# Two-layer graph network kernel: the second layer's block 0 is summed beside the messages, and each projection step sums the next block

## The chip, the cores and the metric

One core of one Trainium2 chip runs the whole program. The time is the device time of one execution in microseconds. The kernel before takes 2986.62 us (median of three runs, 2985.55 to 2993.79).

## The reference, cut to what matters

The program takes 3125 nodes with 256 features and 100,000 edges sorted by destination, and runs two layers. The part that the change touches is in the second layer:

```python
# layer 1, graph part: messages from each edge's source, summed at its destination
h_src = h * norm_src[:, None]
msg = h_src[src]
agg = jax.ops.segment_sum(msg, dst, num_segments=n)
agg = agg * norm_dst[:, None]
out = jax.nn.elu(agg @ weight + bias)
# layer 1, mixer: q, k, v of every node, k-phi^T v summed over all nodes, then per node
q, k, v = x @ Wq + bq, x @ Wk + bk, x @ Wv + bv
kv = jnp.einsum('blhd,blhe->bhde', phi(k), v)
```

Then each node's row goes through the mixer's output projection, a norm, a feed-forward, a norm and the sum with the graph part, and at the end through two of eight experts.

## The kernel before, in words

The nodes are cut into NB = 25 blocks of B = 125, and five blocks (G = 5) make a step, so there are NS = 5 steps. The sum over edges is a dense product: for each destination block, layer 0 has left a table of edge counts between that block and all 25 source blocks (`counts`, 781 KB a block). A block's sum is 25 source blocks by 3 matmuls, since a message is held as three bf16 parts (`part0`, `part1`, `part2`) that add up to the f32 value. These 75 matmuls (`aggregate`, layer 1) accumulate in one PSUM bank, `ps_agg`. POOL loads the count tables into two buffers in turn (`adjacency_in`, `adj1`). After them comes the tail of the block, one round here: POOL's `gather` waits until the last block's tail was used (`tail_free`), loads one tile of edges, says `tail_known`, and fetches the source rows by an indirect load; DVE's `tails` makes a one-hot table from that tile's destinations (`tail_oh_full`); TensorE multiplies the two (`oh_tail`, `xg`), closes the bank (`agg_full`), and ACT's `keep_aggregate` copies the bank out, frees it (`agg_free`) and stores it.

Between the first layer's experts and the second layer's mixer stand two stages:

- **Messages.** ACT, DVE and POOL make the normalised rows and the messages, step by step. ACT says `msg_full` after each step, and POOL, which makes the second and third part of a message (`message_parts`), says `parts_made`. TensorE has no work there but the first transposes.
- **Projection loop.** TensorE's `project1(s)` transposes the five tiles of step s, makes q, k and v (20 matmuls of 512 columns and 20 of 256 in f32 passes), sums block s, and then adds this step's k-phi and v products to `ps_kv` (20 passes, called kv products below). DVE's `project1` adds the biases, and with ACT's Exp makes phi of k (`phi_full`), then the block's tail one-hot, then phi of q, which SP stores (`queries_out`, semaphore `q_free`). ACT's `project1` copies the transposed tiles out of PSUM and runs the Exp.

Each engine runs its instructions in the order in which they are written, so a wait holds back everything behind it. Blocks 0 to 4 are summed in the five projection steps and block 5 (NQ - 1) behind the loop. Then the mixer begins: its place "rows" sums the first half of block 6, and TensorE waits for DVE's `v_full`, which DVE gives after the step's rows and the seven bias rows are loaded (`l_bc`). SP issues these seven loads only once DVE has said `loop_done`, and DVE says that after `q_free` of step 4 and the closed `ps_kv`:

```python
            take(dve, k4_used)
            take(dve, q_free, 16)
            take(dve, sums_full)
            dve.sem_inc(loop_done, 1)
```

Of the kernel before, what the change touches and what calls it, by code (L numbers as in the profile page):

```python
# [27 lines left out]
N, E, D = 3125, 100000, 256  # L28
B = 125
NB = N // B  # L30
# [7 lines left out]
MAXT = NT  # L38
# [7 lines left out]
G = 5  # L46
NS = NB // G
# [17 lines left out]
NQ, NL = NS + 1, 3  # L65
# [3 lines left out]
def take(eng, sem, n=1):  # L69

    eng.wait_ge(sem, n)
    eng.sem_clear(sem)
# [19 lines left out]
def program(nc, a, out):  # L92
    ctx = ExitStack()
    with ctx:
# [10 lines left out]
        ps_agg, ps_kv = banks[0], banks[7]  # L105
# [10 lines left out]
        agg_rows1 = nc.dram_tensor("agg_rows1", (N, D + 1), F32).ap()  # L116
# [29 lines left out]
        tail_n = sb("tail_n", [1, NB], I32)  # L146
# [8 lines left out]
        xg = sb("xg", [B, NB + 1, D + 1])  # L155
        oh_tail, row_tail, col_tail = sb("oh_tail", [B, B]), sb("row_tail", [B, B]), sb("col_tail", [B, NB])
# [579 lines left out]
        def _(pe):  # L736
# [85 lines left out]
            def aggregate(b, par, layer, before, groups=ALL, first=False, last=False, nth=None):  # L822
# [26 lines left out]
                if groups[-1] == GR - 1:  # L849
# [10 lines left out]
                    zero(ps_agg, 260 + NB, False, True).then_inc(agg_full, 1)  # L860

            def turn_slots(groups):

# [177 lines left out]
            def project1(s):  # L1041
# [13 lines left out]
                if s == 0:  # L1055
                    pe.wait_ge(parts_made, NS)
                aggregate(s, s % 2, 1, total, nth=s // 2)
                take(pe, phi_full)
# [12 lines left out]
            pe.wait_ge(l_w1, 48)  # L1071
            total = pe.value_load(cum_tab[0:1, NB:NB + 1], min_val=NB, max_val=MAXT * NB)
            for s in range(NS):
                project1(s)
            zero(ps_kv, 258, False, True).then_inc(sums_full, 1)
            pe.wait_ge(l_c, 16 * 7)
            aggregate(NQ - 1, (NQ - 1) % 2, 1, total, nth=(NQ - 1) // 2)

# [71 lines left out]
        def _(act):  # L1150
# [225 lines left out]
            for s in range(NS):  # L1376
                messages(s)
            with act.Fori(0, NS) as s:
                project1(s)
                keep_aggregate(s, agg_rows1)  # L1380
            act.wait_ge(l_c, 16 * 7)
            act.wait_ge(l_l1, 16 * 4)
            keep_aggregate(NQ - 1, agg_rows1)

# [56 lines left out]
        def _(dve):  # L1441
# [534 lines left out]

            def project1(s):

# [20 lines left out]
                dve.sem_inc(phi_full, 1)  # L1999
                tails(s, 1)  # L2000
                take(dve, q_free, 16)
# [21 lines left out]
            dve.wait_ge(head_stored, 48)  # L2023
            with dve.Fori(0, NS - 1) as s:
                project1(s)
            dve.wait_ge(nodes_stored, 32)
            dve.sem_inc(rowb_used, 1)
            project1(NS - 1)
            take(dve, k4_used)
            take(dve, q_free, 16)  # L2030
# [10 lines left out]
            chain.restart()  # L2041
            tails(NQ - 1, 1)

# [153 lines left out]
```

## Time and profile before

| what | value |
|---|---|
| runs | 2986.62, 2993.79, 2985.55 us |
| the profiled execution's own time | 2994.02 us |
| its span in the trace | 2992.4 us |
| granted TensorE clock, mean over the span | 0.872 of full speed |
| DVE busy | 1159.4 us, 39% |
| ACT busy | 1103.8 us, 37% |
| POOL busy | 542.8 us, 18% |
| DMA | 202.07 MB, 68 GB/s over the span |

Times in the trace count from the span's start. A row of the timeline holds instructions that follow each other, with the time of the first, their busy time together and, in brackets, how long the engine was idle before and who released it. The messages stage runs from 1752 to 1824 us, the projection loop to 1972, and block 5 and the first half of block 6 follow until 1991.

### The profile page before, as it was taken

How to read it: one execution, taken by the hardware profiler on the slowest of the kernel's cores; microseconds unless marked ns; L12 is line 12 of the kernel's file. 1: busy time of each engine (PE TensorE's matmuls, PEld its weight loads, DVE VectorE, ACT ScalarE, POOL GpSimd, SP SyncE). 2: the span in 40 equal slices, each digit the busy share in tenths (PEclk: the TensorE clock that was granted, in tenths of full speed). 3: DMA queues.
4: the chain of work that ended last, by engine and by line, in shares of the span. 5: the costliest groups of instructions: out<-in, count | busy, mean ns of one | idle time of the engine just before them, and what ended most of it. 6: DMA issues, size and time to landing. Idle time of an engine off the chain costs nothing.

```text
span 2992.4 us, 40601 instructions
## 1 busy us (share of the span) xinstructions
PE 2385.0 (80%) x12530; PEld 1931.1 (65%) x12531; DVE 1159.4 (39%) x2546; ACT 1103.8 (37%) x2058; POOL 542.8 (18%) x470
## 2 busy tenths in 40 slices
PE   0777699989889889896679936888788887846887
PEld 0444588877777768775568834666666666635776
DVE  4444577754554544542100034332423334231111
ACT  3122477756555645561223333212222121112232
POOL 1520011100010100102122223010202021113454
PEclk9878799999888898997689977998798897867999
DMA  3321111110110110203332234331222223423443
GB/s 122 95 84 51 30 39 40 44 60 25 34 59 31 53 39 16 75 15 103 101 97 66 64 99 133 95 105 44 75 64 53 71 48 88 122 62 70 82 85 64
DMA packets 163999, 202.07 MB, mean 68 GB/s; under 512 B 55840, under 2 KB 134159, under 8 KB 163860
## 3 DMA queue, kind: packets, MB, share of 16 engines
q0 software_dynamic: 69408, 81.85, 11.8%
q1 hardware_dynamic: 82874, 107.64, 10.9%
q10 hardware_dynamic: 11578, 10.82, 1.1%
q8 instruction: 74, 1.21, 0.2%
q14 instruction: 65, 0.53, 0.1%
HBM read 108.51 MB, written 93.74 MB: 68 GB/s over the span
## 4 chain that ended last, share of the span: by engine, by line
PE 46%; DMA 35%; another core or an unknown queue 7%; ACT 3%; DVE 3%; issue 2%; SPq 2%; POOL 1%; ACTq 0%; DVEq 0%; POOLq 0%
PE bank L738 43%; DMA agg_rows<-agg_t 32%; PE bank L744 3%; POOL w_adj L583 1%; DMA arena<-agg_rows 1%; SPq L411 1%; DMA arena<-in_x 1%; ACT w_qc L1200 0%; DMA xg<-expert_rows 0%; ACT count_a L1200 0%; DMA feat<-row_hot 0%; ACT agg_t L1217 0%; DVE arena L1922 0%; ACT w_adj L1199 0%
## 5 line engine op out<-in xcount | busy, mean ns | idle before, releaser
L738 PE MATMUL bank<-xg,w_adj 125*125 125x256 f32 (+1 forms) x2500 | 583.8, 345 | 1.1 <-DMA w_adj<-counts 1.1
L738 PEld LDWEIGHTS bank<-arena,row_hot 128*125 128x125 f32 x3200 | 428.2, 200 | 87.9 <-issue 67.5
L738 PE MATMUL bank<-arena,row_hot 128*125 128x100 f32 x3200 | 435.6, 283 | 46.9 <-remote 19.6
L738 PEld LDWEIGHTS bank<-xg,w_adj 125*125 125x125 f32 (+1 forms) x2500 | 376.2, 169 | 24.7 <-DMA w_adj<-counts 1.3
L744 PE MATMUL bank<-ident,arena 125*128 125x125 f32 (+1 forms) x650 | 148.3, 355 | 304.2 <-remote 126.3
L738 PE MATMUL bank<-t,w_h 128*128 128x250 f32 (+1 forms) x1184 | 332.5, 435 | 24.4 <-remote 20.3
L744 PEld LDWEIGHTS bank<-ident,arena 125*128 125x128 f32 (+1 forms) x650 | 89.0, 175 | 358.0 <-issue 352.8
L1199 ACT ACTIVATE w_adj<-bank 125x200 f32<-125x200 f32 x400 | 217.3, 543 | 274.6 <-PE bank L738 266.2
L1603 DVE TENSOR_TENSOR row_hot<-iota_all,arena 128x2000 f32<-128x2000 f32 x100 | 223.8, 2238 | 233.7 <-PE bank L738 230.8
L738 PEld LDWEIGHTS bank<-t,w_h 128*128 128x128 f32 x1184 | 234.2, 203 | 120.0 <-issue 68.4
L738 PE MATMUL bank<-w_adj,arena 128*125 128x256 f32 x1024 | 239.9, 392 | 0.0
L1200 ACT ACTIVATE count_a<-bank 125x200 bf16<-125x200 f32 x208 | 227.6, 1094 | 4.0 <-issue 4.0
L738 PEld LDWEIGHTS bank<-w_adj,arena 128*125 128x125 f32 x1024 | 196.7, 196 | 29.7
L1200 ACT ACTIVATE w_qc<-bank 125x200 bf16<-125x200 f32 x192 | 210.1, 1094 | 0.0
L630 POOL DMA_DIRECT2D edge_tail<-in_edges x50 | 27.8, 555 | 823.4 <-PE bank L738 773.1
L738 PE MATMUL bank<-w_adj 125*125 125x256 bf16 x625 | 175.7, 281 | 0.0
L1157 ACT ACTIVATE t<-bank 128x250 f32<-128x250 f32 (+1 forms) x225 | 90.8, 403 | 185.7 <-PE bank L744 183.3
L664 POOL DMA_INDIRECT out_rows<-arena,ids_cur x60 | 119.8, 1997 | 154.4 <-DVEq L1889 119.4
L685 POOL DMA_INDIRECT sorted_in<-arena,pos_cur x75 | 94.4, 1259 | 242.4 <-DVEq L1845 221.4
L1180 ACT ACTIVATE arena<-bank,b_col 128x375 f32<-128x375 f32 (+1 forms) x160 | 83.0, 521 | 118.5 <-PE bank L738 118.4
L633 POOL DMA_INDIRECT xg<-feat,edge_tail x50 | 76.8, 1536 | 263.7 <-DMA edge_tail<-in_edges 156.3
L1263 ACT ACTIVATE arena<-bank,b_col 128x250 f32<-128x250 f32 x136 | 63.5, 469 | 157.3 <-PE bank L738 157.2
(330 smaller groups left out, 3021.2 us busy)
## 6 DMA issues: line engine op xcount, KB each, us to landing
w_adj<-counts POOLq DMA_DIRECT2D x25, 781.2 KB, 8.8
arena<-sorted_in SPq DMA_DIRECT2D x49, 251.0 KB
counts<-count_a SPq DMA_DIRECT2D x13, 781.2 KB
counts<-w_qc SPq DMA_DIRECT2D x12, 781.2 KB
arena<-rows_b SPq DMA_DIRECT2D x5, 1875.0 KB
w_adj<-in_L_ffn_Wd POOLq DMA_DIRECT2D x8, 1024.0 KB, 6.4
w_adj<-in_L_ffn_W POOLq DMA_DIRECT2D x16, 512.0 KB, 5.7
sorted_in<-pad_rows POOLq DMA_DIRECT2D x8, 878.4 KB, 16.8
```

The costliest lines, as they stand in the source:

```text
L411: sp.dma_start(x_big[:, 5 * i:5 * i + 5, :], xv[:, 5 * i:5 * i + 5, :]).then_inc(step_got[i], 16)
L633: pool.indirect_dma_start(xg[:, NB, 0:D], None, feat, bass.IndirectOffsetOnAxis(ap=idx_tail[:, 0:1], axis=0)).then_inc(tail_full, 16)
L664: pool.indirect_dma_start(out, rows_of, y_out[:, i, :], None, bounds_check=N - 1, oob_is_err=False, compute_op=ALU.add).then_inc(y_landed[ ...
L685: pool.indirect_dma_start(sorted_in, bass.IndirectOffsetOnAxis(ap=pos_cur[:, k, i:i + 1], axis=0), src[:, i, :], None).then_inc(scattered, 16)
L738: return pe.matmul(o, w, r, start=first, stop=last, skip_group_check=not check)
L744: return pe.transpose(ps[:, at:at + n], src, ident[0:n, 0:n])
L1157: chain(act.activation(t4[:, k:k + n, B * i:B * i + B], ps_t[i % 2][:, 0:n * B].rearrange("p (k n) -> p k n", k=n), ACT.Copy))
L1180: last = act.activation(ht[:, slot + j, lo:hi], ps_h[half][:, 0:hi - lo], func, bias=b(j))
L1199: act.activation(wide(adj[par], g), ps[:, :, 0, :, :], ACT.Copy)
L1200: last = act.activation(wide(count_cur[par], g), ps[:, :, 1, :, :], ACT.Copy)
L1263: act.activation(ht[:, j, 0:PT], ps_u[j % 4][:, 0:PT], ACT.Gelu, bias=b(e, j)).then_inc(unit_done[j % 4], 1)
L1603: tt(row_hot[:, k % 2, :, :], iota_all[:, :].unsqueeze(1).to_broadcast([128, GJ, B]), src[1].to_broadcast([128, GJ, B]), ALU.is_equal)
```

## The change

`first_sums` opens the sums' bank right behind the experts and sums block 0 source step by source step: it waits for `parts_made` of each of the five steps and issues the 15 matmuls of that step's five source blocks. `project1(0)` then begins. Behind its projections stands `first_tail`, which adds block 0's tail and closes the bank; then `project1(0)` sums block 1, and each further step s sums block s + 1. The block behind the loop is gone. ACT keeps two sums in step 0 and one in each later step, and DVE makes two tail one-hots in step 0. POOL and SP are unchanged.

```diff
+            def first_sums():
+                open_sums()
+                pe.wait_ge(adj_in[0], 16)
+                for s in range(NS):
+                    pe.wait_ge(parts_made, s + 1)
+                    for c in range(G * s, G * s + G):
+                        mm(ps_agg[0:B, 0:D + 1], adj1[0][:, c, 0:B], part0[:, c, :], False, False, False)
+                        mm(ps_agg[0:B, 0:D], adj1[0][:, c, 0:B], part1[:, c, :], False, False, False)
+                        mm(ps_agg[0:B, 0:D], adj1[0][:, c, 0:B], part2[:, c, :], False, False, False)
+                zero(ps_agg, 16, False, False).then_inc(adj_used[0], 1)
+
+            def first_tail(before):
+                n = pe.value_load(tail_n[0:1, 0:1], min_val=1, max_val=MAXT)
+                with pe.Fori(0, n) as c:
+                    take(pe, tail_oh_full)
+                    pe.wait_ge(tail_full, pe.snap((before + c + 1) * 16))
+                    mm(ps_agg[0:B, 0:D + 1], oh_tail[:, :], xg[:, NB, 0:D + 1], False, False, False).then_inc(tail_free, 1)
+                zero(ps_agg, 260 + NB, False, True).then_inc(agg_full, 1)
...
                 if s == 0:
-                    pe.wait_ge(parts_made, NS)
-                aggregate(s, s % 2, 1, total, nth=s // 2)
+                    first_tail(total)
+                aggregate(s + 1, (s + 1) % 2, 1, total, nth=(s + 1) // 2)
                 take(pe, phi_full)
...
+            first_sums()
             for s in range(NS):
                 project1(s)
             zero(ps_kv, 258, False, True).then_inc(sums_full, 1)
             pe.wait_ge(l_c, 16 * 7)
-            aggregate(NQ - 1, (NQ - 1) % 2, 1, total, nth=(NQ - 1) // 2)
...
-            with act.Fori(0, NS) as s:
+            project1(0)
+            for b in range(2):
+                keep_aggregate(b, agg_rows1)
+            with act.Fori(1, NS) as s:
                 project1(s)
-                keep_aggregate(s, agg_rows1)
+                keep_aggregate(s + 1, agg_rows1)
...
-            keep_aggregate(NQ - 1, agg_rows1)
...
-            with dve.Fori(0, NS - 1) as s:
-                project1(s)
+            project1(0)
+            tails(1, 1)
+            with dve.Fori(1, NS - 1) as s:
+                project1(s + 1)
             dve.wait_ge(nodes_stored, 32)
             dve.sem_inc(rowb_used, 1)
-            project1(NS - 1)
+            project1(NS)
...
-            tails(NQ - 1, 1)
```

How the instructions stand on TensorE is printed below; L72 is the line of a wait, and the semaphores that a row waits for are in brackets. The first place is the beginning of the stage, right behind the last expert. Before:

```order
1505 L738 MATMUL bank<-zero_r,zero_w 128x258
1506 L1072 TENSOR_LOAD cum_tab [waits w_qkv1_loaded]
1507 L1072 ISA x2
1508 L72 ISA [waits turned_ps_free0,messages1_full]
1509 L744 MATMUL bank<-ident,arena 128x125 x2
1510 L72 ISA [waits turned_ps_free1]
1511 L744 MATMUL bank<-ident,arena 128x125 x2
```

And with the change, where the last of the five groups of 15 (its first matmul waits for the parts) ends and the first transpose follows:

```order
1508 L72 ISA [waits agg_ps_free]
1509 L738 MATMUL bank<-zero_r,zero_w 128x285
1510 L738 MATMUL bank<-xg,w_adj 125x257 [waits message_parts_made,adjacency_in0]
...
1570 L738 MATMUL bank<-xg,w_adj 125x257 [waits message_parts_made]
...
1585 L738 MATMUL bank<-zero_r,zero_w 128x16
1586 L72 ISA [waits turned_ps_free0,messages1_full]
1587 L744 MATMUL bank<-ident,arena 128x125 x2
1588 L72 ISA [waits turned_ps_free1]
1589 L744 MATMUL bank<-ident,arena 128x125 x2
```

The transposes and projections of step 0 now stand behind all 75 matmuls of block 0, the last 15 of which wait for the last message parts.

The second place is the end of step 0's projections on TensorE, with the change. Before, the last projection (`w_qc,t`) was followed by the 75 matmuls of block 0, and its tail came behind them:

```order
1616 L738 MATMUL bank<-w_qc,t 125x256 x2
1617 L876 TENSOR_LOAD tail_n
1618 L876 ISA x2
1619 L877 UNCONDITIONAL_BRANCH
1620 L72 ISA [waits tail_onehot_full]
1621 L879 ISA
1622 L738 MATMUL bank<-xg,oh_tail 125x257 [waits tail_rows_full]
1623 L877 REGISTER_ALU
1624 L877 COMPARE_AND_BRANCH
1625 L738 MATMUL bank<-zero_r,zero_w 128x285
1626 L72 ISA [waits agg_ps_free]
1627 L738 MATMUL bank<-zero_r,zero_w 128x285
```

Two waits now stand between the projections and the next 75 matmuls: that for the tail's one-hot and that for the bank.

The third place is the end of the loop on TensorE, behind the last kv products. Before, block 5 stood between them and the mixer (its 75 matmuls follow the last row here):

```order
2117 L738 MATMUL bank<-arena 128x129 x10
2118 L738 MATMUL bank<-zero_r,zero_w 128x258
2119 L72 ISA [waits agg_ps_free,w_c_loaded]
2120 L738 MATMUL bank<-zero_r,zero_w 128x285
```

With the change the mixer's loop begins there, and its first work is the first half of block 6:

```order
2204 L738 MATMUL bank<-arena 128x129 x10
2205 L738 MATMUL bank<-zero_r,zero_w 128x258
2206 L1162 UNCONDITIONAL_BRANCH [waits w_c_loaded]
2207 L72 ISA [waits agg_ps_free]
2208 L738 MATMUL bank<-zero_r,zero_w 128x285
2209 L830 ISA
...
2243 L72 ISA [waits vector_stage_full]
2244 L72 ISA [waits turned_ps_free0]
2245 L744 MATMUL bank<-ident,arena 128x125 x2
```

## Rows read from the trace of the kernel before

**Rows 1.** Page, part 1: busy time, share of the span, instructions.

```profile
PE 2385.0 (80%) x12530; PEld 1931.1 (65%) x12531; DVE 1159.4 (39%) x2546; ACT 1103.8 (37%) x2058; POOL 542.8 (18%) x470
```

**Rows 2.** Timeline of PE, steps 0 and 1: start us, us, instructions [idle <-releaser].

```profile
1776.97 1.09 PE L744 MATMUL bank<-ident,arena 125*128 125x125 f32 x4 [29.51 <-ACTq L1356]
1819.94 2.05 PE L744 MATMUL bank<-ident,arena 125*128 125x125 f32 x6 [41.88 <-ACTq L1159]
1821.78 15.05 PE L738 MATMUL bank<-w_qc,t 128*125 128x512 f32 x40
...
1845.49 0.70 PE L738 MATMUL bank<-xg,oh_tail 125*125 125x257 f32 x2
...
1846.34 2.50 PE L738 MATMUL bank<-arena 125*128 125x129 f32 x20
1848.67 0.59 PE L744 MATMUL bank<-ident,arena 125*128 125x125 f32 x4
...
1852.58 14.83 PE L738 MATMUL bank<-w_qc,t 128*125 128x512 f32 x40
```

**Rows 3.** Timeline of POOL, the last of the five message parts.

```profile
1821.80 2.52 POOL L616 TENSOR_TENSOR w_adj<-row_hot,xg 125x1280 bf16<-125x1280 f32 x1
```

**Rows 4.** Timeline of DVE in step 0, the tail's one-hot.

```profile
1843.55 0.29 DVE L1652 TENSOR_SCALAR oh_tail<-iota_all,dst_tail 125x125 f32<-125x125 f32 x1
```

**Rows 5.** Three stretches: length, busy by engine (instructions), PEclk, DMA share, GB/s.

```profile
1777.00:1819.00 42.00, 1.07 (x4) 0.68 (x4) 27.91 (x53) 25.88 (x49) 26.72 (x17) 0.50 0.34 120
...
1822.00:1827.00 5.00, 5.00 (x10) 2.45 (x10) 1.04 (x2) 0.38 (x1) 2.32 (x1) 0.62 0.35 124
...
1985.20:1990.70 5.50, 5.45 (x33) 5.21 (x33) 0.00 (x0) 0.00 (x0) 1.16 (x1) 0.69 0.34 118
```

**Rows 6.** Timeline of PE, step 4, block 5 and the mixer's beginning.

```profile
1945.51 14.63 PE L738 MATMUL bank<-w_qc,t 128*125 128x512 f32 x40
...
1969.64 2.50 PE L738 MATMUL bank<-arena 125*128 125x129 f32 x20
...
1982.02 0.69 PE L738 MATMUL bank<-xg,oh_tail 125*125 125x257 f32 x2 [1.05 <-DVE oh_tail L1652]
...
1983.80 0.29 PE L738 MATMUL bank<-zero_r,zero_w 1*128 1x285 bf16 x1 [0.87 <-ACTq L1218]
...
1993.71 1.09 PE L744 MATMUL bank<-ident,arena 125*128 125x125 f32 x4 [3.05 <-remote]
```

**Rows 7.** Timeline of POOL, gather for block 1, and landing of the indirect loads.

```profile
1846.96 0.58 POOL L630 DMA_DIRECT2D edge_tail<-in_edges  x1 [7.25 <-PE bank L738]
1852.33 1.24 POOL L633 DMA_INDIRECT xg<-feat,edge_tail  x1 [4.78 <-remote]
...
DMA to landing us min/median/max: 4.2/5.3/8.7
```

**Rows 8.** Timelines of DVE and SP between step 4 and the mixer.

```profile
1967.49 1.49 DVE L2003 SCALAR_TENSOR_TENSOR count_a<-arena 125x1280 f32<-125x1280 f32 x1 [0.19 <-remote]
...
1993.52 1.49 DVE L2060 TENSOR_TENSOR arena<-arena,bias 125x1280 f32<-125x1280 f32 x1 [11.77 <-DMA arena<-rows_b]
...
1969.12 0.27 SPq L506 DMA_DIRECT2D rows_b<-count_a  x1
1978.13 0.28 SPq L519 DMA_DIRECT2D bias<-in_L_gnn_bias  x1
...
1982.62 2.63 SPq L519 DMA_DIRECT2D bias<-in_L_mix_ln_b  x1
```

**Rows 9.** Timelines of PE and DVE, step 2 and the beginning of step 3.

```profile
1879.25 0.59 PE L744 MATMUL bank<-ident,arena 125*128 125x125 f32 x4
...
1891.27 8.00 PE L738 MATMUL bank<-w_qc,t 128*125 128x512 f32 x24 [1.01 <-DVE arena L1984]
...
1911.11 0.59 PE L744 MATMUL bank<-ident,arena 125*128 125x125 f32 x4
...
1888.01 1.49 DVE L2003 SCALAR_TENSOR_TENSOR count_a<-arena 125x1280 f32<-125x1280 f32 x1 [13.65 <-remote]
```

More of the change, by code:

```diff
@@ L1975, in nodes1, with project1 @@
                 chain.restart()
-            def project1(s):
+            def project1(b):
                 take(dve, k4_used)
@@ L1999, in project1 @@
                 dve.sem_inc(phi_full, 1)
-                tails(s, 1)
+                tails(b, 1)
                 take(dve, q_free, 16)
```

## The prediction

> **What bounds the kernel now.** I read the busy times first: TensorE is busy 80% of the span, the next engine 39% [rows 1]. So TensorE is the first suspect, but a share is a mean over stages, and the change moves work between two of them. The timeline of TensorE around them tells more. In the messages stage it stands still: two tiles are transposed at 1776.97, and the third waits 41.88 us, until 1819.94 [rows 2]. The projections of step 0 then run from 1821.78 to 1836.83, block 0's 75 matmuls fill the time to its tail at 1845.49, the kv products follow at 1846.34, and step 1 begins at 1848.67 [rows 2]. Inside the loop TensorE is the bound. A block costs 1845.49 - 1836.83 = 8.7 us with its opening, 0.115 us a matmul.
>
> At the loop's end I looked at who releases TensorE, since removing work there pays only if TensorE is late. Its projections of step 4 end at 1945.51 + 14.63 = 1960.14, the kv products at 1972.1, block 5 runs to its tail at 1982.02, half of block 6 from 1983.80, and then it is idle for 3.05 us, until the mixer's first transpose at 1993.71 [rows 6]. The rows of DVE and SP name the real chain: DVE ends phi of q at 1968.98, SP stores it at 1969.12, the store has landed by 1978.1, when SP issues the first of seven bias loads; the last is issued from 1982.62 to 1985.25, and DVE starts the mixer at 1993.52, 0.19 us before TensorE [rows 8]. DVE's row names an old load of rows as releaser, which was issued long before; the bias loads are what can have come last. So from the end of step 4's projections to the mixer there are 1993.71 - 1960.14 = 33.6 us whatever TensorE does, and block 5 lies in their shadow.
>
> **The change, part by part.** I follow TensorE from the last message parts to the end of step 0. Before, that end was 1848.67.
>
> 1. *Block 0 beside the messages.* The first 60 matmuls fall in the 41.88 us of idleness and cost nothing; if that cover were gone they would cost 60 x 0.115 = 6.9 us. The last 15 wait for POOL's last part, ready at 1824.32 [rows 3]. They take 15 x 0.115 = 1.7 us at full clock, 3.5 us at the half clock (1.2 GHz) that TensorE was granted through this stage, 0.50 [rows 5]. I take the level that the row shows, 3.5: 1827.8.
> 2. *Transposes.* They now stand behind this. In step 1 it took 1852.58 - 1848.67 = 3.9 us from the first transpose to the first projection, because ACT loads its Copy table only once a tile is there [rows 2]. In step 0 that was hidden, now it is not. With transposes at half clock (1.09 us for four against 0.59) I take 4.2: 1832.0.
> 3. *Projections.* 15.0 us, as in both steps [rows 2]: 1847.0 instead of 1836.83.
> 4. *The tail's one-hot.* DVE made it at 1843.84, 7.0 us after the last projection, since phi of k and two Exp stand before it [rows 2, 4]. Before, the 75 matmuls covered this. Now nothing does, for the tail comes first: 1854.0. The order of work can't shorten this wait, since DVE's own order is unchanged up to there.
> 5. *Tail, closing, and the bank.* Block 1 needs the same bank, and ACT must copy it out first. From tail to reopening it took 1983.80 - 1982.02 = 1.8 us [rows 6]: 1855.8. ACT is free by then; its Exp is what the one-hot waited for.
> 6. *Block 1.* 8.7 us at full clock. After the pause in point 4 I expect part of it at half clock: after the pause before block 6, 33 matmuls took 5.5 us at a mean clock of 0.69 [rows 5], where 33 x 0.115 = 3.8 would do. So +1.7: 1866.2.
> 7. *Block 1's tail rows.* POOL may fetch them only after block 0's tail is used, at 1854.7. From there the row shows 0.8 us to the edge load, 5.4 to the indirect load, and 5.3 (median, 4.2 to 8.7) to its landing [rows 7]: 11.4 us, so 1866.1, level with point 6. Between no wait and 3.4 us I take 0.5, near the median: 1866.7. Before, a whole step lay between two tails.
> 8. *Tail and kv products*, 1848.67 - 1845.49 = 3.2 us [rows 2]: step 0 ends at 1869.9, which is **21.2 us later**.
> 9. *Steps 1 to 4.* The same instructions in the same order, with the next block's count table and tail. Count tables are issued at the same distance, a step ahead. One stall goes: before, DVE waited 13.65 us for an old store, until 1888.01, and TensorE 1.01 us for DVE, so that the step from 1879.25 took 31.9 us where the loop's first full step took 30.6 [rows 2, 9]. That store waited behind SP's weight loads, which do not move, and DVE now reaches it some 20 us later. I take the whole difference, **-1.3 us**.
> 10. *Behind the loop.* Block 5's 75 matmuls, tail and reopening go, from 1972.1 to 1983.80, 11.7 us of TensorE. The chain of store, `loop_done` and bias loads is unchanged, so TensorE does half of block 6 and idles until 33.6 us after its projections: **0**. What may go is contention: block 7's table came in beside the last bias loads and will come earlier now. At most 2 us of the 8.3 us from the last bias issue to DVE's start [rows 8]; I count none and keep 2 for the range. Below zero it can hardly cost anything.
> 11. *ACT's and DVE's second pieces in step 0* (one more copy, one more one-hot) run while TensorE is in block 1, and POOL and SP issue what they did. The mixer's passes behind are the same work; nothing there waits for an absolute time. 0.
>
> Sum: 21.2 - 1.3 + 0 = **+19.9 us**. The profiled execution would take 2994.0 + 19.9 = 3013.9 us. It was 7.4 us above the median of the runs, so against the median the forecast is 2986.6 + 19.9 = **3006.5 us**, 0.7% slower. A difference under 0.3%, 9 us, can't be told from none here.
>
> The Trainium skill, DMA: Bandwidth & Descriptors, "Latency and other measured facts", gives some 2 us as a DMA's fixed cost. By that estimate block 1's rows would be there about 6 us after the first tail, and the sum would be 0.5 us smaller; the 5.4 and 5.3 us of the rows speak against it, and they hold.
>
> The Trainium skill, TensorE: Matmul & The Clock Gate, "Why this matters for your kernels", advises against gaps between bursts of matmuls, for the clock falls in them. That speaks against this change, which opens such a gap in point 4. The 1.7 us of point 6 come from the row of block 6, and the trace agrees with the rule there; without it the sum would be 1.7 us smaller.
>
> Bounds. Below: full clock in points 1, 2 and 6 makes 1.8 + 0.3 + 1.7 = 3.8 us less, of which the tail rows (11.4 us after the first tail) give back about 1.5, and 2 us of point 10: +15. Above: the lower clock through all projections of step 0. In 1822 to 1827, mostly at half clock, 10 matmul rows ran in 5 us [rows 5], against 40 in 15; that would be at most 10 us more, and tail rows 3.4 us late: +33.
>
> **The rivals.**
> - *Block 5 was on the path after all (slower by less than can be told).* If the mixer's first transpose waited for TensorE itself, the 11.7 us of point 10 would come back: 19.9 - 11.7 = +8.2, 2994.8 us, and with the lower bounds less. It decides if the chain from step 4's projections to DVE's start is shorter than 33.6 - 11.7 = 21.9 us. For it: TensorE was idle only 3.05 us there. Against it: DVE's and SP's rows add up without TensorE. Chance 0.09.
> - *Slower still, by clock and late rows.* Point 1's bursts keep the clock down through step 0's projections and block 1, and the indirect load lands late: +28, 3015 us. For it: half clock for 42 us. Against it: step 0's projections began at the lower level before, too, and still took 15.05 us [rows 2, 5]. Chance 0.12.
> - *The stages interleave as meant.* If DVE's one-hot and block 1's rows did not hold up TensorE, only the late start of the projections would be paid, 1832.0 - 1821.78 = 10.2 us, and with block 5's 11.7 and the 1.3 back it would be -2.8: 2983.8 us, no change. The Trainium skill, Perfetto Trace Analysis, "Optimization Strategy", says that interleaving stages with different limits may help; the time for it is this rival's. Against it stands the order of DVE: the one-hot comes after phi of k. Chance 0.03.
>
> **How the numbers follow.** The forecast itself, with bounds of +15 to +25, has 0.74, and 0.02 is left for a gain that no row shows. The range goes from 2997 to 3017: it leaves out the third rival, most of the first and the far end of the second, and takes in the run-to-run spread of some 4 us. Slower by over 0.3% is the forecast, the second rival and a part of the first: 0.88. Within 0.3%: 0.10. Faster: 0.02.
>
> **What would show it.** In the profile after: 15 matmuls on `xg,w_adj` after each message part; the first projection of step 0 near 1832 and its last near 1847; a pause of some 7 us on TensorE released by DVE's `oh_tail`, one of 0.9 us released by ACT, perhaps one by the tail rows; step 1 beginning near 1870; steps of 30.4 to 30.6 us; and after the loop a pause of 15 to 17 us before the mixer's first transpose (3.05 + 11.7, and what block 6 lost to its pause and the lower clock), still 33.6 us after step 4's projections. I am wrong if that last distance shrinks by over 3 us, or if step 0 ends before 1862.

## The result and the profile after

| | before | after |
|---|---|---|
| runs, median (lowest to highest) | 2988.51 us (2979.30 to 3001.97), 20 runs | 3001.89 us (2984.74 to 3011.39), 20 runs |
| ratio after to before, on record | | 1.0030 (95%: 1.0018 to 1.0043) |
| span of the profiled execution | 2992.4 us | 2999.6 us |
| granted clock, mean | 0.872 | 0.874 |

The changed kernel is slower, as forecast, but not by 19.9 us. The recorded ratio makes it 9.0 us (5.4 to 12.8). It isn't the quotient of the two medians, which lie 13.4 us apart, just beyond that interval; so read the size as some 9 to 13 us. The direction was right; half to two thirds of the amount came.

The spans can't be subtracted. In the changed kernel's execution the experts ended 10.8 us earlier than in that of before, at 1736.4 against 1747.2 us, though nothing there was changed. So I count from the end of POOL's last message part, 1824.32 before [rows 3] and 1810.81 + 2.51 = 1813.32 after, and cut at TensorE's first transposes:

| stretch | before | after | difference | forecast |
|---|---|---|---|---|
| last message part to step 1 | 24.35 | 47.01 | +22.66 | +21.2 |
| steps 1 to 3 | 92.80 | 82.82 | -9.98 | -1.3 |
| step 4 and loop's end, to the mixer | 52.24 | 49.29 | -2.95 | 0 |
| first two passes of the mixer | 29.91 | 33.76 | +3.85 | 0 |
| sum | 199.30 | 212.88 | +13.58 | +19.9 |

The first row is where the forecast looked, and it holds. The second and third are where it failed: each of steps 1 to 4 is some 3 us shorter (2.75 to 4.25), and the forecast had only 1.3 us for all of them, from one stall.

Timeline of TensorE after, from the last of the five groups of block 0 into step 1 (start, us, instructions, [idle <-releaser]); it answers to [rows 2]:

```profile
1813.42 0.69 PE L738 MATMUL bank<-xg,w_adj 125*125 125x257 bf16 x2 [7.13 <-POOLq L617]
...
1816.95 1.09 PE L744 MATMUL bank<-ident,arena 125*128 125x125 f32 x4
...
1820.16 13.90 PE L738 MATMUL bank<-w_qc,t 128*125 128x512 f32 x40
1842.40 1.21 PE L738 MATMUL bank<-xg,oh_tail 125*125 125x257 f32 x2 [8.34 <-DVE oh_tail L1675]
...
1844.75 0.41 PE L738 MATMUL bank<-zero_r,zero_w 1*128 1x285 bf16 x1 [0.79 <-ACTq L1239]
...
1857.14 0.70 PE L738 MATMUL bank<-xg,oh_tail 125*125 125x257 f32 x2 [1.53 <-DMA xg<-feat,edge_tail]
...
1860.33 0.59 PE L744 MATMUL bank<-ident,arena 125*128 125x125 f32 x4
1861.40 0.43 PE L744 MATMUL bank<-ident,arena 125*128 125x125 f32 x2 [0.49 <-ACTq L1180]
...
1862.96 13.14 PE L738 MATMUL bank<-w_qc,t 128*125 128x512 f32 x40
```

All three waits that the prediction named are there, in their order: the one-hot 8.34 us, the bank 0.79, the tail rows 1.53. But look at the last two rows. In step 1, TensorE pauses 0.49 us between its first transposes and the next, and the projections take 13.14 us; before, they took 14.83 [rows 2], behind a pause of 1.76:

```profile
1851.03 0.43 PE L744 MATMUL bank<-ident,arena 125*128 125x125 f32 x2 [1.76 <-ACTq L1159]
```

ACT's timeline says what the pause was. Before, in step 1:

```profile
1849.16 1.28 ACT L1157 ACT_TABLE_LOAD   x1 [2.16 <-PE bank L744]
1850.45 0.38 ACT L1157 ACTIVATE t<-bank 128x250 f32<-128x250 f32 x1
```

After, in steps 0 and 1:

```profile
1835.91 1.28 ACT L1385 ACT_TABLE_LOAD   x1 [15.04 <-DVEq L2018]
1837.20 2.43 ACT L1385 ACTIVATE arena<-arena 125x1280 f32<-125x1280 f32 x2
1844.16 0.39 ACT L1238 ACTIVATE agg_t<-bank 125x257 f32<-125x257 f32 x1 [4.53 <-DMA agg_rows<-agg_t]
...
1860.83 0.38 ACT L1178 ACTIVATE t<-bank 128x250 f32<-128x250 f32 x1 [2.17 <-PE bank L744]
```

Before, every step began with a load of ACT's table; after, there is one load in front of step 0's Exp, and none in steps 1 to 4. The listing of ACT's instructions shows the same thing. Before, the loop's body begins with the load (`1282 L1157 ACT_TABLE_LOAD`, the first row behind the loop's branch and its wait). With the change the row `1292 L1385 ACT_TABLE_LOAD` stands in step 0's peeled copy, and the loop behind `1304 L1402 UNCONDITIONAL_BRANCH` holds none. The page agrees, with four instructions fewer on ACT than in [rows 1] (2054 for 2058):

```profile
PE 2377.7 (79%) x12530; PEld 1926.4 (64%) x12531; DVE 1160.3 (39%) x2546; ACT 1100.6 (37%) x2054; POOL 544.4 (18%) x470
```

The pause fell by 1.27 us, about the load's length. The other 1.7 us lie in the projections, and the three stretches of step 1 before show why (length, busy by engine, PEclk, DMA share, GB/s):

```profile
1850.70:1852.50 1.80, 1.04 (x6) 0.59 (x6) 0.00 (x0) 1.01 (x4) 0.17 (x1) 1.00 0.34 119
1852.50:1857.00 4.50, 4.50 (x11) 2.42 (x11) 0.69 (x1) 0.64 (x2) 1.64 (x2) 0.62 0.70 201
1857.00:1867.00 10.00, 10.00 (x32) 5.74 (x31) 4.08 (x8) 0.00 (x0) 0.00 (x0) 1.00 0.42 126
```

Right behind the pause the granted clock fell to a mean of 0.62, so that most of 4.5 us ran at 1.2 GHz. After the change the clock stays at 1.00 there:

```profile
1862.00:1874.00 12.00, 11.73 (x38) 6.90 (x39) 4.39 (x8) 1.15 (x3) 1.82 (x2) 1.00 0.86 211
```

The Trainium skill, ScalarE: Activation LUTs, "What ACT_TABLE_LOAD costs", gives 1283 ns for the load and some 1380 ns for a drain, 2.66 us a switch. The trace agrees with the first, 1.28 us. It doesn't show the second: ACT had been idle before the load, and its next instruction begins 0.01 us behind it.

At the loop's end it went as forecast. TensorE, SP and DVE after:

```profile
1992.44 1.09 PE L744 MATMUL bank<-ident,arena 125*128 125x125 f32 x4 [17.41 <-remote]
...
1967.48 0.27 SPq L506 DMA_DIRECT2D rows_b<-count_a  x1
1976.81 0.28 SPq L519 DMA_DIRECT2D bias<-in_L_gnn_bias  x1
...
1982.57 2.82 SPq L519 DMA_DIRECT2D bias<-in_L_mix_ln_b  x1
...
1992.25 1.49 DVE L2084 TENSOR_TENSOR arena<-arena,bias 125x1280 f32<-125x1280 f32 x1 [13.73 <-DMA arena<-rows_b]
```

Step 4's projections end at 1958.91, and the mixer's first transpose follows 33.53 us later, against 33.6 before [rows 6, 8]. TensorE now idles 17.41 us where it idled 3.05. Block 5 was taken out of a shadow. Which transfer DVE waits for in the end isn't shown: its row names the load of the nodes' rows (`rows_b`), the prediction the bias rows.

### The profile page after: what moved, and what is told of

Its sections match the earlier page's. It is cut to its first block, busy times and chain, and to the rows that moved or that the text cites. A ratio compares the mean times of both kernels' runs of the same rounds, so it can differ in the third digit from the quotient of the medians.

```text
span 2999.6 us, 40584 instructions
## 1 busy us (share of the span) xinstructions
PE 2377.7 (79%) x12530; PEld 1926.4 (64%) x12531; DVE 1160.3 (39%) x2546; ACT 1100.6 (37%) x2054; POOL 544.4 (18%) x470
## 4 chain that ended last, share of the span: by engine, by line
PE 43%; DMA 36%; another core or an unknown queue 7%; ACT 5%; DVE 3%; issue 2%; SPq 2%; POOL 1%; ACTq 0%; DVEq 0%; POOLq 0%
PE bank L738 40%; DMA agg_rows<-agg_t 33%; PE bank L744 3%; SPq L411 1%; POOL w_adj L583 1%; DMA arena<-agg_rows 1%; ACT arena L1299 1%; ACT count_a L1221 0%; DMA xg<-expert_rows 0%; ACT w_qc L1221 0%; DMA feat<-row_hot 0%; ACT agg_t L1238 0%; ACT w_adj L1220 0%; DVE arena L1945 0%
## 5 line engine op out<-in xcount | busy, mean ns | idle before, releaser
L738 PE MATMUL bank<-xg,w_adj 125*125 125x256 f32 (+1 forms) x2500 | 590.7, 348 | 62.8 <-POOLq L617 62.8
L1284 ACT ACTIVATE arena<-bank,b_col 128x250 f32<-128x250 f32 x136 | 63.7, 471 | 156.6 <-PE bank L738 156.5
```

What stands on the lines that cost most here:

```text
L738: return pe.matmul(o, w, r, start=first, stop=last, skip_group_check=not check)
L1284: act.activation(ht[:, j, 0:PT], ps_u[j % 4][:, 0:PT], ACT.Gelu, bias=b(e, j)).then_inc(unit_done[j % 4], 1)
```

## The experiments

Each kernel was timed beside the kernel before on the same chip, in 6 to 12 executions; where one execution is said, there is no ratio. The medians of before were 2990.41, 2987.32 and 2986.64 us in the three series. "Step 0" stands for the stretch from the last message part to step 1's first transpose.

**Peeling ACT's loop alone, on the kernel before.** TensorE's order stays that of before.

```diff
-            with act.Fori(0, NS) as s:
+            project1(0)
+            keep_aggregate(0, agg_rows1)
+            with act.Fori(1, NS) as s:
                 project1(s)
                 keep_aggregate(s, agg_rows1)
```

> The kernel before, with nothing changed but ACT's projection loop: step 0 is written out ahead of the loop, which runs over steps 1 to 4. Theory: the loop then begins with the Exp table in place and ACT loads no table in steps 1 to 4, so the first transpose of a step is followed by its first projection after 2.6 us instead of 3.9, TensorE's pause falls from 1.76 to 0.5 us, its clock does not fall, the projections take 13.1 instead of 14.8 us, and a step takes 27.6 instead of 30.6 us: 12 us less in four steps, some 1 us in step 0, about 2975 us against 2988. Rival (the shorter steps of the change come from TensorE's order or from the tail one step ahead): steps stay at 30.6 us and the time at 2988.

Measured: 2986.04 us, ratio 0.9995 (0.9975 to 1.0015), no gain that can be told, where some 2975 was expected. The table loads of steps 1 to 4 are gone and steps 1 and 3 take 27.61 us, as with the change. But step 2 takes 40.21 us, which eats the gain. TensorE and DVE there, and SP's queue up to it:

```profile
1880.75 10.07 PE L738 MATMUL bank<-w_qc,t 128*125 128x512 f32 x24 [10.27 <-DVE arena L1986]
...
1877.48 1.49 DVE L2005 SCALAR_TENSOR_TENSOR count_a<-arena 125x1280 f32<-125x1280 f32 x1 [19.93 <-remote]
...
1822.91 31.87 SPq L497 DMA_DIRECT2D wn<-in_L_gnn_weight  x1
...
1865.24 14.32 SPq L506 DMA_DIRECT2D rows_b<-count_a  x2
```

DVE may write step 1's queries only once step 0's have been stored. SP issues that store behind seven weight loads, the first of which kept its queue 31.87 us. Counted from the last message part (1811.88 here), DVE went on after 65.6 us, and before, from 1888.01 [rows 9], after 63.7: an almost fixed time. Before, TensorE came late enough to lose only 1.01 us to it [rows 9]; here it begins step 2 4.4 us earlier and is 3 us faster inside it, and the stall ends 2 us later, so it loses 10.27. So the peeling is the cause of the shorter steps, and it doesn't pay by itself in this kernel; the change, which starts its steps some 20 us later, passes under the stall.

**The loads put back into the changed kernel.** One dummy operation leaves ACT with the Sqrt table before the loop, as the messages did.

```diff
                 keep_aggregate(b, agg_rows1)
+            table(ACT.Sqrt)
             with act.Fori(1, NS) as s:
```

> The changed kernel with ACT's Sqrt table loaded between step 0 and the loop, so that the loop is again entered with another table than it leaves. Theory: the load at the first copy of steps 1 to 4 is back, the steps take 30.6 us again, and the kernel is 12 us slower than the changed one: ratio to before 1.007, near the 19.9 us that were forecast. Rival (the load is not what made the steps shorter): steps stay at 27.6 us, ratio 1.003.

Measured: 3010.77 us, ratio 1.0062 (1.0040 to 1.0083), 18.5 us slower than before. The load is back in each step, the steps take 30.30, 30.45 and 30.56 us, and step 1's projections, behind a pause of 1.87 us, are slow again:

```profile
1874.00 1.28 ACT L1178 ACT_TABLE_LOAD   x1 [0.30 <-PE bank L744]
...
1877.63 14.24 PE L738 MATMUL bank<-w_qc,t 128*125 128x512 f32 x40
```

This is the kernel that the prediction had costed, and the 19.9 us of its sum lie inside the interval of what it measured (12 to 25 us). By stages it agrees too: from the last message part to the mixer's first transpose it took 187.9 us, 18.5 more than before. That a loop which is entered with one table and left with another needs a load in every pass is my reading of the two listings and of this pair of kernels; no row says it.

**Block 5's 75 matmuls left out of the kernel before.** Its sums are not computed.

```diff
-                        for c in range(NB * max(g - 1, 0) // 15, NB * g // 15):
+                        for c in range(0 if empty else NB * max(g - 1, 0) // 15, 0 if empty else NB * g // 15):
...
-            aggregate(NQ - 1, (NQ - 1) % 2, 1, total, nth=(NQ - 1) // 2)
+            aggregate(NQ - 1, (NQ - 1) % 2, 1, total, nth=(NQ - 1) // 2, empty=True)
```

> The kernel before without the 75 matmuls of block 5 behind the loop (its tail and its store stay, so the sums of block 5 are left out). Theory: the mixer's first transpose waits for the chain store, loop_done, bias loads, and stays 33.6 us behind the last projection of step 4, with TensorE idle some 8 us longer: same time as before. Rival (block 5 was on the path): 8.7 us less and the distance falls to 25 us.

Measured: 2990.02 us, ratio 1.0001 (0.9986 to 1.0017). Taking away 8.7 us of TensorE's work gains nothing; the wait for the tail's one-hot takes its place, and the mixer begins 35.3 us behind step 4's projections, not sooner than the 33.6 of before:

```profile
1969.35 1.22 PE L738 MATMUL bank<-xg,oh_tail 125*125 125x257 f32 x2 [9.41 <-DVE oh_tail L1652]
...
1982.92 0.64 PE L744 MATMUL bank<-ident,arena 125*128 125x125 f32 x4 [3.33 <-remote]
```

By itself this leaves the tail of block 5 in TensorE's way, and TensorE idle for 3.33 us only, as before. Together with the changed kernel, in which nothing of block 5 is left there and the distance is still 33.53 us, it refutes the rival with block 5 on the path.

**The changed kernel without block 0's tail product and one-hot.** The tail of block 0 is not added.

```diff
                 with pe.Fori(0, n) as c:
-                    take(pe, tail_oh_full)
                     pe.wait_ge(tail_full, pe.snap((before + c + 1) * 16))
-                    mm(ps_agg[0:B, 0:D + 1], oh_tail[:, :], xg[:, NB, 0:D + 1], False, False, False).then_inc(tail_free, 1)
+                    pe.sem_inc(tail_free, 1)
...
-                tails(b, 1)
+                if not isinstance(b, int) or b > 0:
+                    tails(b, 1)
...
             dve.wait_ge(head_stored, 48)
+            take(dve, tail_known)
             project1(0)
```

> The changed kernel with block 0's tail product and its one-hot left out (the tail rows are fetched and awaited as before). Theory: the pause of 8.3 us between step 0's projections and block 1 goes, and with it the lower clock in block 1 (2 us): step 0 ends 9 to 11 us sooner, the whole kernel is about as fast as before. Rival (the pause only hides another wait, for block 0's tail rows or block 1's): a wait of 5 us or more appears in its place and 3 us at most are gained.

Measured: 2991.29 us, ratio 1.0008 (0.9991 to 1.0025). Step 0 takes 42.38 us, 4.6 less than with the change. The 8.34 us of the one-hot gave way to another wait, for ACT's copy of the bank:

```profile
1838.50 0.29 PE L738 MATMUL bank<-zero_r,zero_w 1*128 1x285 bf16 x1
1844.60 0.41 PE L738 MATMUL bank<-zero_r,zero_w 1*128 1x285 bf16 x1 [5.81 <-ACTq L1238]
```

ACT's copy stands behind its table load and both Exp. The one-hot is only the last of two waits that end close together, and behind it 5.81 of its 8.34 us remain.

The last line of the edit costs time of its own. The word `tail_known`, which the one-hot no longer takes, is now taken ahead of all of DVE's work in step 0, so DVE stands still until the edge load of block 0 has landed. The projections wait 1.60 us for it and take 15.80 us where they took 13.90:

```profile
1829.52 0.07 DVE L2003 MEMSET arena<- 125x10 f32 x1 [28.10 <-remote]
```

So the 4.6 us are a lower bound for what this wait was worth; with the projections at 13.90 it would be 6.5, an estimate.

**The same, with ACT's copy of block 0's sums ahead of the two Exp.**

```diff
                 copy_turned(2)
+                if isinstance(s, int):
+                    keep_aggregate(0, agg_rows1)
                 for n in (1, 0):
...
-            for b in range(2):
-                keep_aggregate(b, agg_rows1)
+            keep_aggregate(1, agg_rows1)
```

> As e4 (block 0's tail product and one-hot left out), and ACT copies block 0's sum out before its two Exp of step 0 instead of behind them. In e4 TensorE waited 5.8 us for that copy. Theory: the pause between the projections of step 0 and block 1 falls to about 1 us, the clock stays up, and step 0 ends some 8 us sooner than in e4, 12 us sooner than in the changed kernel: some 3 us faster than before. Rival (block 1's tail rows, which come 11 us after the last use, bind next): 2 to 3 us of that are given back.

Measured: 2983.30 us, ratio 0.9990 (0.9964 to 1.0015). Step 0 takes 37.71 us, 9.3 less than with the change. The projections wait 2.71 us for DVE, again through the line with `tail_known`, part of them runs slower (17.80 us in all, for 13.90), and 0.78 us remain at the bank:

```profile
1834.44 9.70 PE L738 MATMUL bank<-w_qc,t 128*125 128x512 f32 x24 [2.71 <-DVE arena L2007]
...
1845.14 0.29 PE L738 MATMUL bank<-zero_r,zero_w 1*128 1x285 bf16 x1 [0.78 <-ACTq L1238]
```

With both waits away, the way from the last message part to the mixer's third transposition is 199.0 us, that of before 199.3. Step 0 is still 13.4 us longer than before (some 9.5 by estimate, with the projections at 13.90), since transposes and projections now stand behind the messages, and the shorter steps give back 12.9. So of the 22.7 us by which step 0 had grown, taking both waits away gave back 9.3 (13 by that estimate), and what is left and the shorter steps cancel. In time the kernel can't be told from before.

**Peeling with `loop_done` said earlier, on the kernel before.** DVE gives it right behind the last phi of q, ahead of its waits for the store and for `ps_kv`.

```diff
+            dve.sem_inc(loop_done, 1)
             take(dve, k4_used)
             take(dve, q_free, 16)
             take(dve, sums_full)
-            dve.sem_inc(loop_done, 1)
```

> The kernel before with ACT's loop peeled (as e1) and DVE's loop_done given before the three waits behind the loop, right after phi of q of step 4. Theory: SP issues the bias loads 9 us earlier, the chain that starts the mixer ends before block 5 and half of block 6 do, and the mixer's first transpose follows TensorE's own work, 30 us behind step 4's projections instead of 33.6 (e1: 34.4 with the last step): 3 to 4 us less than e1. Rival (the mixer waits for an old load of rows, as its row says, not for the biases): no change against e1.

Measured: 2978.67 us, ratio 0.9979 (0.9955 to 1.0003). From step 4's first transpose to the mixer's it took 51.13 us, no less than the 50.17 of the peeling alone: the stretch I had expected to shrink did not, since block 5's tail rows now came late. What did shrink is the mixer's first pass, 14.15 us for 17.72, and TensorE no longer idles before it; that the one comes of the other is my reading:

```profile
1968.36 1.22 PE L738 MATMUL bank<-xg,oh_tail 125*125 125x257 f32 x2 [5.32 <-DMA xg<-feat,edge_tail]
...
1977.57 0.59 PE L744 MATMUL bank<-ident,arena 125*128 125x125 f32 x4
```

**The same, with step 0's query store ahead of SP's weight loads.** This tests the account of the 10.27 us stall.

```diff
+            take(sp, q_full)
+            sp.dma_start(rows(rows_b[:, 2 * D:3 * D], 0), q1).then_inc(q_free, 16)
             sp.dma_start(wn[:, :, :], wview(a["L1_gnn_weight"])).then_inc(l_c, 16)
...
-            with sp.Fori(0, NS - 1) as s:
+            with sp.Fori(1, NS - 1) as s:
                 queries_out(s)
```

> As e5, and SP stores step 0's queries ahead of the seven weight loads instead of behind them. Theory: in e1 the table load was taken out of four steps, 12 us, but DVE's wait for that store grew and stopped TensorE for 10.3 us in step 2; with the store ahead, step 2 takes 27.6 us like the others instead of 40.2, and the kernel is some 12 us faster than e5 and 15 us faster than before, ratio 0.995. Rival (the store itself is slow, or the weight loads then hold back step 1's store by as much): a stall of 10 us moves to step 3.

Measured: 2961.81 us, ratio 0.9922 (0.9892 to 0.9951), some 23 us faster than before, and the fastest of all. Steps 1 to 3 take 27.61, 27.60 and 27.61 us: the stall in step 2 is gone. Step 2's projections on TensorE, and the store on SP:

```profile
1866.72 13.14 PE L740 MATMUL bank<-w_qc,t 128*125 128x512 f32 x40
...
1833.87 22.50 SPq L498 DMA_DIRECT2D rows_b<-count_a  x1
```

Even in front, the store keeps SP's queue 22.50 us, but now nobody waits for it, and the weight load behind it keeps the queue only 5.37 us: the long hold goes with the place in the queue, not with the weight load. Of the 23 us, the stretches of the table give 13.8 in the profiled execution (185.5 against 199.3 us). The rest lies outside them, where executions of one kernel differ by as much (below), and I can't assign it.

**A pause without a table.** The peeled kernel before, with a Copy of 1.25 us on an unused tile ahead of the first copy of each of steps 1 to 4 (one execution).

```diff
                     take(act, t_act[i % 2])
+                    if pause and i == 0:
+                        idle = cut(17800, 1250)
+                        chain(act.activation(idle, idle, ACT.Copy))
...
-                copy_turned(2)
+                copy_turned(2, pause=not isinstance(s, int))
```

> As e1 (no table load in steps 1 to 4), with one ACT copy of 125x1250 elements, some 1.2 us, put where the table load was: after the wait for the first transposed tile. Theory: the pause of TensorE alone costs the clock; the projections take 14.8 us again instead of 13.1 and steps 1, 3 and 4 take some 30.4 us, of which 1.3 are the pause and 1.7 the clock. Rival (the table load itself slows something else): steps take 27.6 + 1.2 = 28.8 us.

Measured: 2991.36 us. The pause on TensorE is 1.76 us again, in all four steps. Steps 1 and 3 take 28.88 and 28.89 us, 1.3 more than with no pause, and their projections run at full clock; in steps 2 and 4 the clock fell. TensorE in steps 1, 3 and 4, then, in a fence of their own, two stretches of step 1:

```profile
1846.97 0.43 PE L744 MATMUL bank<-ident,arena 125*128 125x125 f32 x2 [1.76 <-ACTq L1162]
...
1916.67 13.14 PE L738 MATMUL bank<-w_qc,t 128*125 128x512 f32 x40
...
1945.56 14.61 PE L738 MATMUL bank<-w_qc,t 128*125 128x512 f32 x39
```

```profile
1844.60:1848.40 3.80, 1.60 (x11) 0.92 (x10) 0.07 (x1) 2.46 (x5) 0.24 (x1) 1.00 0.34 120
1848.40:1852.40 4.00, 4.00 (x13) 2.23 (x13) 1.12 (x2) 0.69 (x2) 1.58 (x2) 1.00 0.64 184
```

So 1.3 us of the 3.0 are the pause, whether the clock falls or not. The other 1.7 are the clock's, and a pause of this length may cost them or not: it fell in every step of the kernels that had the loads, in two of four here, and in none whose pause was 0.49 us.

**Both kernels a second time** (one execution each, nothing edited), to see what repeats.

> The kernel before, unchanged, for a second trace. What the readings by stage rest on should repeat to some 1 to 2 us: 24.4 us from the last message part to step 1, 30.6 us a step with the table load, 52 us from step 4 to the mixer's first transpose; the rest of the spread between executions should lie ahead of the messages and behind the mixer's first pass.

> The changed kernel, unchanged, for a second trace: 47.0 us from the last message part to step 1, 27.6 us a step, 49.3 us from step 4 to the mixer's first transpose. If these repeat, the difference between the two kernels from the last message part to the mixer is 9.7 us, whatever the whole times of the two executions are.

Measured: 2966.54 and 2999.46 us. Step 0 took 24.33 and 45.81 us, the steps 30.58, 31.07, 30.58 and three times 27.6, the way from step 4 to the mixer 52.39 and 48.57. The mixer's first two passes took 29.93 and 32.67 us. Every stretch of the table repeats to 1.2 us, and this pair's sum is +11.0 us where the first pair's was +13.6. Outside the table nothing repeats so well. The same kernel before reached its last message part at 1824.3 us in one execution and at 1805.8 in the other. One profiled execution is good for a stage and not for the whole; the whole is judged by the ratio alone.

**The changed kernel with `loop_done` earlier and the store in front**, to see whether the idle 17 us can be had.

```diff
+            dve.sem_inc(loop_done, 1)
             take(dve, k4_used)
...
-            dve.sem_inc(loop_done, 1)
...
+            take(sp, q_full)
+            sp.dma_start(rows(rows_b[:, 2 * D:3 * D], 0), q1).then_inc(q_free, 16)
...
-            with sp.Fori(0, NS - 1) as s:
+            with sp.Fori(1, NS - 1) as s:
```

> The changed kernel with loop_done given early and step 0's store ahead of the weight loads (as in e9). Theory: the store's place changes nothing here, since DVE comes to that wait late anyway; the bias loads are issued 9 us earlier, TensorE has nothing behind the loop but half of block 6, so the mixer begins 24 to 25 us behind step 4's projections instead of 33.5: 9 us less than the changed kernel, about the time of before, and some 20 us more than e9. Rival (what holds the mixer is not the biases): the distance stays at 33.5 us.

Measured: 2989.38 us, ratio 1.0007 (0.9986 to 1.0029). The distance from step 4's projections (end 1963.29) to the mixer fell to 30.8 us, 2.7 less; I had expected 9. SP and TensorE, then four stretches between them:

```profile
1972.23 2.31 SPq L521 DMA_DIRECT2D bias<-in_L_gnn_bias  x1
...
1981.12 0.96 SPq L521 DMA_DIRECT2D bias<-in_L_mix_ln_b  x1
...
1994.11 1.09 PE L746 MATMUL bank<-ident,arena 125*128 125x125 f32 x4 [14.71 <-remote]
```

```profile
1984.00:1986.00 2.00, 0.00 (x0) 0.00 (x0) 0.00 (x0) 0.00 (x0) 0.00 (x0) 0.62 0.91 253
1986.00:1988.00 2.00, 0.00 (x0) 0.00 (x0) 0.00 (x0) 0.00 (x0) 0.00 (x0) 0.50 0.99 187
1988.00:1990.00 2.00, 0.00 (x0) 0.00 (x0) 0.00 (x0) 0.00 (x0) 0.00 (x0) 0.50 0.44 114
1990.00:1992.00 2.00, 0.00 (x0) 0.00 (x0) 0.00 (x0) 0.00 (x0) 0.00 (x0) 0.50 0.32 101
```

The first bias load is issued 0.4 us behind the store and not 9.3, but the last has left SP's queue only at 1982.08 and DVE starts at 1993.92. The store, the tail's rows, block 7's count table and the biases are in flight together there, with the DMA engines up to 99% busy, and that this contention takes back most of the early issue is my reading: from 1988 on they are 44 and 32% busy, and DVE still doesn't start. The two kernels with peeling and the early `loop_done` agree: DVE starts the mixer 31.1 and 32.0 us behind step 4's projections, and 34.2 in the kernel that was only peeled. So the time of the bias loads counts for some 2 to 3 us; what holds the rest, these transfers or the row load that DVE's row names, was not tried.

## Why the prediction was right in direction and wrong in size

By its own points, with the changed kernel's first execution:

- **Point 1**, the last 15 matmuls, 3.5: 3.63. The 60 beside the messages cost nothing: from the experts' end to the last message part it took 76.8 to 77.3 us with them and without.
- **Point 2**, transposes, 4.2: 3.21. There was no table load in step 0's copies either. The forecast had taken step 1's distance, which holds one, and had seen that it does ("ACT loads its Copy table"), without asking why it is loaded there.
- **Point 3**, projections, 15.0: 13.90. They began at the lower clock and soon had the full one.
- **Point 4**, the one-hot, 7.0: 8.34. The table load, 1.28 us, had moved in front of the first Exp, on the very path that the one-hot waits for.
- **Point 5**, tail and bank, 1.8: 2.35, at the lower clock; the wait for ACT was 0.79 (0.87 forecast).
- **Point 6**, block 1, 10.4: 10.86. The clock had fallen to 0.50 over the pause of point 4 and came back after 1848.99 (0.98 in the next 4 us). That it falls in such a gap is the rule that the prediction quotes from the Trainium skill (TensorE: Matmul & The Clock Gate, "Why this matters for your kernels"), and this trace agrees. The prediction found the rule in its row of block 6, too, but the page speaks of longer gaps than the 1.05 and 0.87 us ahead of that row [rows 6]. So the price was near by a row of another kind.
- **Point 7**, tail rows, 0.5: 1.53. The edge load came 0.78 us after the first tail's use and the indirect load 5.29 later, as in [rows 7]; from its issue to TensorE's start it took 7.46 us, within the 4.2 to 8.7 shown and above the median.
- **Point 8**: 3.19 (3.2). Sum of step 0: 47.01 for 45.6. The errors of the points are up to 1.3 us each and in part cancel.
- **Point 9, "The same instructions in the same order": this step failed.** TensorE's instructions in steps 1 to 4 were the same, but ACT's were not. The diff's `with act.Fori(1, NS)` looked like a change of a bound; it took the table load out of the loop, and ACT's listing would have shown the row gone; the prediction looked at the order on TensorE alone. The four steps measured 2.75 to 4.25 us less each (the 4.25 in step 2, with its stall), -12.9 us together, where the forecast had -1.3. So this step alone put the sum 11.6 us too high. Putting the loads back gave +18.5 us.
- **Point 10**, behind the loop, 0: right. The distance is 33.53 us, and leaving block 5's matmuls out of the kernel before gained nothing. The reason given for it is only half shown: issuing the biases 9 us earlier, in the changed kernel, brought the mixer 2.7 us forward, so they aren't the whole chain.
- **Point 11**, nothing in the mixer: its first two passes took 3.9 us longer. It is the clock again. In all these executions but two, TensorE idled before the mixer and began it at 1.2 GHz or nearly; what differs is how soon the full clock comes back. Four to twelve microseconds behind the mixer's first transpose before, and then eight to sixteen behind it after (stretches as above):

```profile
1997.70:2001.70 4.00, 3.19 (x15) 2.79 (x16) 1.78 (x9) 0.76 (x2) 0.00 (x0) 0.73 0.00 0
2001.70:2005.70 4.00, 3.64 (x31) 3.45 (x32) 2.40 (x13) 0.00 (x0) 0.00 (x0) 1.00 0.02 4
```

```profile
2000.40:2004.40 4.00, 3.66 (x17) 3.35 (x16) 2.52 (x12) 0.00 (x0) 0.00 (x0) 0.50 0.00 0
2004.40:2008.40 4.00, 4.00 (x31) 4.00 (x30) 0.87 (x4) 0.00 (x0) 0.00 (x0) 0.78 0.03 6
```

It is tempting to blame the 17.41 us of idleness, but the runs don't: the peeled kernel idled only 2.22 us and took 17.72 us for the first pass, and the one without one-hot and with the early copy idled 16.69 and took 15.15, as before. What decides it stays open. It may belong to the change all the same, since the kernel before took 15.1 us for this pass both times and the changed one 17.7 and 16.9. Only with no idleness at all, in the two kernels with peeling and the early `loop_done`, was it 14.2 both times.

So the sum goes from 19.9 by +1.5 (step 0), -11.6 (point 9) and +3.9 (point 11) to +13.6 us by stages, or +11.0 in the second pair. The measured difference is 9.0 (5.4 to 12.8), or 13.4 between the medians. What remains between them is within what stages outside do from one execution to the next. In the prediction's upper bound, the 10 us for the lower clock through the projections don't follow from its row: 10 matmul rows in 5 us make 40 in 20, 5 us more than 15.

Of the rivals, block 5 on the path named nearly the right time (+8.2) for the wrong reason, and an experiment was needed to say so: the measured +9 alone would have spoken for it. The rival with the clock down through step 0's projections did not come. The stages did not interleave as meant: two waits stand in the way, which cost 9.3 us or somewhat more, and even without them step 0 is 13.4 us longer (9.5 by estimate), near the 10.2 that this rival had for the late start of the projections.

## What to carry to other kernels

When an iteration is peeled off a loop, compare the instruction lists of every engine whose loop is rewritten, not only of the one that bounds, and look for table loads that appear, vanish or move: here one of 1.28 us in a loop cost 3.0 us a step on another engine. When a wait is costed, ask what is second: of the one-hot's 8.3 us only 4.6 came back (6.5 by estimate, without what the edit itself cost), since the bank's copy ended nearly as late. Look, too, for what an experiment's own edit adds, as that wait for `tail_known` did. And a stall bound to an absolute time (a store behind bulk loads on one queue) swallows what is gained ahead of it. Moving work off the bounding engine pays only where that engine is last; the idle 17 us at the loop's end were spent waiting for transfers.

## What was not expected of the hardware

- The same pause of 1.76 us on TensorE lowered the granted clock behind it in some steps and not in others of one execution: 13.14 us for the projections in one, and 14.61 for 39 of 40 in another. A pause of 0.49 us never did.
- After idleness the full clock came back 4 to 8 us after TensorE's start in three executions (a mean of 0.68 to 0.73 in that stretch, then 1.00), 8 to 12 us after it in five, and 12 to 16 in three (0.78 in the changed kernel's), and how long the engine had idled, from 2.0 to 17.4 us, didn't decide which.
- One issue of a DMA can keep SP's queue for 31.87 us (the first of seven weight loads) and for 22.50 us (a store put in front of them, after which the same weight load took 5.37); everything behind it on that queue waits so long.
